# Sorting the edges of a four-layer graph network: column pieces of 96, 489, 489 and 489, each prepared right ahead of its ranks

## The reference, cut to what matters

```python
h = jnp.maximum(_layernorm(x, axis=-1), 0.0)
x = x + _L0_gnn_ref(h, src, dst, ...)                            # attention: softmax over the edges of a node
...
x = x + _L1_gnn_ref(h, ..., edge_index, edge_type_8)             # relations: means per type, in both directions
...
x = x + _L2_gnn_ref(h, edge_attr_16, ..., edge_index, 0, 4)      # sum over edges by src, then an MLP
...
x = x + _L3_gnn_ref(h, edge_index_t, edge_attr_6, ...)           # sum over edges by dst
```

## Time and profile before

| | us |
|---|---|
| time, median of 3 runs (15910.03 to 15919.94) | 15916.97 |
| time of the profiled execution | 15913.28 |
| its span | 15911.1 |
| busy: POOL / PE / DVE / PEld / ACT | 11144.0 / 10293.0 / 9384.4 / 8268.7 / 2592.3 |

### The profile page before, as it was taken

How to read it: one execution, slowest core, us unless ns; L and a number is a source line. 1 busy time by engine, 2 the same in 40 slices (tenths; PEclk the granted TensorE clock), 3 DMA queues, 4 the chain that set the end, 5 groups by cost and what they waited for, 6 DMA issues and landing times. The chain is left out here.

```text
span 15911.1 us, 207629 instructions
## 1 busy us (share of the span) xinstructions
PE 10293.0 (65%) x60197; PEld 8268.7 (52%) x60197; DVE 9384.4 (59%) x30337; ACT 2592.3 (16%) x6666; POOL 11144.0 (70%) x11474
## 2 busy tenths in 40 slices
PE   6766647777777775555554555553777768777777
PEld 2222226666666663344444444443666665666666
DVE  9977758888788777755555555554333332333331
ACT  0011114444444442211111111111000002000000
POOL 4777777777777776677777777774777760677773
PEclk9966669999999997755555555555555555555555
DMA  2011122222222224322223222223222232222223
GB/s 80 11 46 52 48 62 69 69 68 69 69 70 69 69 69 110 112 58 57 57 57 54 62 61 62 61 61 55 61 62 62 62 54 65 64 58 58 58 57 39
DMA packets 675304, 988.05 MB, mean 62 GB/s; under 512 B 232206, under 2 KB 473564, under 8 KB 674076
## 3 DMA queue, kind: packets, MB, share of 16 engines
q0 software_dynamic: 392896, 680.65, 18.5%
q1 hardware_dynamic: 281308, 294.11, 6.1%
HBM read 795.08 MB, written 178.86 MB: 61 GB/s over the span
## 5 line engine op out<-in xcount | busy, mean ns | idle before, releaser
L1528 DVE TENSOR_TENSOR acc<-banks,acc 128x145 f32 (+1 forms) x3328 | 1011.3, 304 | 2712.3 <-PE banks L1512 2345.9
L722 POOL DMA_INDIRECT far_sum_dst<-table_h,recs_sum_dst x1664 | 1578.1, 948 | 1026.0 <-DMA recs_sum_dst<-rec_dst 519.2
L621 POOL DMA_INDIRECT rec_dst<-stage_dst_sort,row_dst_sort x1563 | 1569.9, 1004 | 694.5 <-issue 475.6
L722 POOL DMA_INDIRECT far_sum_src<-table_h,recs_sum_src x1664 | 1576.5, 947 | 652.2 <-issue 426.3
L722 POOL DMA_INDIRECT far_att<-table_qv,recs_att x1664 | 1626.5, 977 | 532.5 <-issue 506.5
L722 POOL DMA_INDIRECT far_rel_dst<-table_xw,recs_rel_dst x1664 | 1590.0, 956 | 562.8 <-issue 506.9
L1404 DVE TENSOR_TENSOR acc<-banks,acc 128x128 f32 x3328 | 969.8, 291 | 1694.6 <-PE banks L1359 1331.7
L722 POOL DMA_INDIRECT far_rel_src<-table_xw,recs_rel_src x1664 | 1588.5, 955 | 537.4 <-issue 506.8
L1511 PE MATMUL banks<-far_sum_src,hot_sum_src 128*128 128x128 f32 x3328 | 1285.8, 490 | 745.7 <-issue 579.5
L1511 PE MATMUL banks<-far_sum_dst,hot_sum_dst 128*128 128x128 f32 x3328 | 1286.2, 490 | 640.4 <-issue 579.6
L1359 PE MATMUL banks<-far_rel_dst,hot_s_rel_dst 128*128 128x128 f32 x3328 | 851.4, 438 | 1045.1 <-DVE share_rel_dst L1394 708.2
(11 more groups left out here) (304 smaller groups left out, 23233.4 us busy)
## 6 DMA issues: line engine op xcount, KB each, us to landing
table_xw<-xw_rel_tables SPq DMA_DIRECT2D x98, 512.0 KB, 2.7
far_att<-table_qv,recs_att POOLq DMA_INDIRECT x1664
far_rel_dst<-table_xw,recs_rel_dst POOLq DMA_INDIRECT x1664
far_rel_src<-table_xw,recs_rel_src POOLq DMA_INDIRECT x1664
far_sum_src<-table_h,recs_sum_src POOLq DMA_INDIRECT x1664
far_sum_dst<-table_h,recs_sum_dst POOLq DMA_INDIRECT x1664
rec_dst<-stage_dst_sort,row_dst_sort POOLq DMA_INDIRECT x1563
rec_src<-moved_att,row_src POOLq DMA_INDIRECT x1248
```

The lines of the kernel that those rows point to most:

```text
L621: e.indirect_dma_start(out=flat_dst, out_offset=bass.IndirectOffsetOnAxis(ap=row["dst"][:, c + i:c + i + 1], axis=0), in_=stage["dst"][:, ...
L722: e.indirect_dma_start(out=self.far[:, g % RING, t, :], out_offset=None, in_=table, in_offset=bass.IndirectOffsetOnAxis(ap=index, axis=0)) ...
L1528: e.tensor_tensor(acc[:, bass.ds(at[t], 1), :], bank(g0, t).unsqueeze(1), acc[:, bass.ds(at[t], 1), :], ALU.add).then_inc(k.s_sum, 1)
```

## The change

The four quarters of 391, 391, 391 and 390 columns become four pieces of 96, 489, 489 and 489. The `begin`, parts and copies of a piece are no longer done for all columns at once ahead of all ranks, but for each piece right ahead of its 98 units. On TensorE the three rounds of a piece stand ahead of that piece's matmuls. GpSimd's chunk waits for the piece that holds its last column; 96 columns are three whole chunks.

```diff
-QUARTERS = 4
-QN = -(-ET // QUARTERS)
+PIECES = 4
+BEGINS = [0, *(96 + i * (ET - 96) // (PIECES - 1) for i in range(PIECES))]
+QN = max(b - a for a, b in zip(BEGINS, BEGINS[1:]))
...
-def quarter(q):
-
-    return q * QN, min(QN, ET - q * QN)
+def piece(q):
+
+    return BEGINS[q], BEGINS[q + 1] - BEGINS[q]
+
+
+def piece_of(c):
+    return sum(c >= b for b in BEGINS[1:])
...
+                def parted(q):
+
+                    c, m = piece(q)
+                    mine = begin[:, c:c + m]
+                    follow()
+                    then(e.scalar_tensor_tensor(out=mine, in0=mine, scalar=base[:, 0:1], in1=k.psum[q][0:W, 0:m], op0=ALU.add, op1=ALU.subtract))
+                    for j in range(3):
+                        follow()
+                        then(e.tensor_copy(part[:, j, c:c + m], mine))
+                        if j < 2:
+                            follow()
+                            then(e.tensor_tensor(mine, mine, part[:, j, c:c + m], ALU.subtract))
+                    at["parts", s, q] = n
+
+                    for g in range(GROUPS3):
+                        e.wait_ge(s_placed, (i * PIECES + q) * GROUPS3 + g + 1)
+                        e.tensor_copy(packed[:, g, c:c + m], k.psum[q][:, 0:m]).then_inc(s_packed, 1)
+
                 for u in range(AHEAD):
                     marked(u)
                 for u, (q, w) in enumerate(units):
-                    c, m = quarter(q)
+                    c, m = piece(q)
+                    if w == 0:
+                        parted(q)
...
                 for u, (q, w) in enumerate(units):
-                    c, m = quarter(q)
+                    c, m = piece(q)
+                    if w == 0:
+                        e.wait_ge(s_rank, at["parts", s, q])
+                        for g in range(GROUPS3):
+                            if g:
+                                e.wait_ge(s_packed, (i * PIECES + q) * GROUPS3 + g)
+                            for j in range(3):
+                                at0 = 3 * W3 * g - j + 2
+                                t = e.matmul(k.psum[q][:, 0:m], spread[:, at0:at0 + P], part[:, j, c:c + m], start=(j == 0), stop=(j == 2))
+                            t.then_inc(s_placed, 1)
+                        e.wait_ge(s_packed, (i * PIECES + q + 1) * GROUPS3)
...
-                e.wait_ge(s_row, (c + n - 1) // QN + 1)
+                e.wait_ge(s_row, piece_of(c + n - 1) + 1)
```

More of the change, by code:

```diff
@@ L245, in sort_edges @@
         spread, triple = sb("spread", [W, 3 * P], BF16), sb("triple", [P, W3 + 1], BF16)
-        over_part, over_packed = sb("over_part", [P, 3 * ET // 2 + 1]), sb("over_packed", [P, GROUPS3 * QUARTERS * QN // 2])
+        over_part, over_packed = sb("over_part", [P, 3 * ET // 2 + 1]), sb("over_packed", [P, -(-GROUPS3 * ET // 2)])
         begun = sb("begun", [P, ET])
@@ L250, in sort_edges @@
         part = over_part[0:W, :].bitcast(BF16)[:, 0:3 * ET].rearrange("w (j t) -> w j t", j=3)
-        packed = over_packed[:, :].bitcast(BF16).rearrange("p (g q n) -> p g q n", g=GROUPS3, q=QUARTERS)
+        packed = over_packed[:, :].bitcast(BF16)[:, 0:GROUPS3 * ET].rearrange("p (g n) -> p g n", g=GROUPS3)
         total = sb("total", [W, 1])
@@ L298, in sort_edges @@
         chunks = W // C7
-        units = [(q, w) for q in range(QUARTERS) for w in range(W)]
+        units = [(q, w) for q in range(PIECES) for w in range(W)]
         U = len(units)
@@ L347, in ranks @@
                 e.wait_ge(s_counted, (i + 1) * W)
-                for q in range(QUARTERS):
-                    c, m = quarter(q)
+                for q in range(PIECES):
+                    c, m = piece(q)
                     follow()
@@ L365, in ranks @@
                 then(e.tensor_scalar(base[:, :], k.psum[4][0:W, 0:1], float(P), None, ALU.mult))
-                follow()
-                for q in range(QUARTERS):
-                    c, m = quarter(q)
[L369 to L384, removed]
                 def marked(u):
                     q, w = units[u]
-                    c, m = quarter(q)
+                    c, m = piece(q)
                     if i * U + u >= 5:
@@ L414, in ranks @@
                                            op0=ALU.mult, op1=ALU.add).then_inc(s_row, 1)
-                e.wait_ge(s_row, QUARTERS * (i + 1))
+                e.wait_ge(s_row, PIECES * (i + 1))
                 if not i:
@@ L501, in tensor @@
                 e.matmul(k.psum[4][0:W, 0:1], k.before[0:W, 0:W], tiles[:, :], start=True, stop=True).then_inc(s_base, 1)
[L502 to L511, removed]
-                for u, (q, w) in enumerate(units):
-                    c, m = quarter(q)
+                for u, (q, w) in enumerate(units):
+                    c, m = piece(q)
+                    if w == 0:
[8 more added lines that the diff above has]
+                        e.wait_ge(s_packed, (i * PIECES + q + 1) * GROUPS3)
                     g, j = divmod(w, W3)
-                    if u == 0:
-                        e.wait_ge(s_packed, (i + 1) * GROUPS3 * QUARTERS)
                     e.wait_ge(s_begun, i * U + u + 1)
@@ L520, in tensor @@
                     bank = k.psum[4 + u % 4][:, 0:m]
-                    e.matmul(bank, triple[:, j:j + 1].to_broadcast([P, P]), packed[:, g, q, 0:m], start=True, stop=False)
+                    e.matmul(bank, triple[:, j:j + 1].to_broadcast([P, P]), packed[:, g, c:c + m], start=True, stop=False)
                     e.matmul(bank, before_b[:, :], mark[:, (i * U + u) % 5, 0:m], start=False, stop=True).then_inc(s_unit, 1)
```

## The result

The changed kernel takes 15951.27 us (median of 11 runs, 15937.88 to 15965.41), the kernel before in the same comparison 15916.5 us (11 runs, 15898.07 to 15943.88). The ratio is 1.0021, with a 95% interval of 1.0014 to 1.0029: slower by 35 us (22 to 46 by the interval), where 39 were forecast, 15956 from 15917. The profiled execution took 15953.65 us, with a span of 15951.9.

What follows compares the result with a forecast made beforehand. VectorE's `ranks`, then staging and 1083 writes, were taken to bound the sort. Terms of 3.3, 12.4, 2.8 and 1.5 made 20.0 us a side, +40 on 15917, less one: 15956, range 15938 to 15972.

Steps and rivals of the forecast that it cites:

- What bounds the sort: Sort's chain: VectorE's `ranks` until 826.83, 25.8 us of staging, then 1083 writes; first 480 writes beside it, 28 us slack.
- Parts, copies, refill: Preparing each piece on VectorE and TensorE: begins and parts +3.3, copies +12.4, refill +2.8 us a side.
- Units: VectorE's mark and copy pairs: wider and narrower units cancel, 38 against 38 us, leaving +1.5 us a side.
- floor: In 96-column units each copy waits for the copy before: 0.33 us where the line gives 0.31, +1.5 us a side.
- the line of 1.31 ns: Price per column of a VectorE unit: 489 columns take 0.13 us more than 391, 96 columns 0.39 less.
- The start: GpSimd's writes get their first rows at about 145, starting some 52 us earlier.
- The end: The early start all becomes waiting; the writes' end moves by +40 us, just as far as `normalize`.
- A: The forecast itself: `ranks` grows by 32 to 50 us and the end with it, 15949 to 15967; chance 0.61.
- B: Clock is up in TensorE's rounds and the floor is nothing: +22 us, 15939, up to 15949; chance 0.22.
- C: Small units on VectorE don't overlap: 0.46 us instead of 0.33, adding 25 us, 15981; chance 0.09.
- D: GpSimd's earlier start carries through to the end: 52 us less, 15865; chance 0.05.
- E: Nothing moves: more than half of the added waits in `ranks` are hidden, 15917 to 15939; chance 0.03.

Runs made afterwards that it cites:

- e1: Changed kernel with GpSimd's writes held back until the second piece has its rows; 15956.75 us, ratio 1.0023 to the kernel before.
- e12: Changed kernel with all pieces' begins up front and a piece's three spread rounds in three banks without waits between; 15946.06 us, ratio 1.0013 to the kernel before.
- e7: As e12, plus unused matmuls on TensorE ahead of the later pieces' rounds, on the chip running 28% longer; ratio 0.9988 to the kernel before.
- e10: Kernel before with pieces of 96, 489, 489, 489, all prepared up front, and 17 chunks staged ahead instead of 14; 15863.29 us, ratio 0.9969.
- e11: Kernel before with only 17 chunks staged ahead of the first window instead of 14; 15904.58 us, ratio 0.9985.
- e3: Changed kernel with four equal pieces, each still prepared right ahead of its ranks; 15945.61 us, ratio 1.0017 to the kernel before.

## Why the prediction was right

**What bounds the sort.** Right: VectorE's `ranks`, then staging, then the writes. 826.83 to 864.98 is +38.15, and the writes resume +37.98. e1 confirms the slack on the other side: 92 us of later start moved the resumption by 1.2. The stop was forecast at some 120 us and took 116.65.

**Parts, copies, refill: +18.5 a side forecast.** The preparation from the first begin to the first copied unit took 106.94 to 126.24 before, 19.3 us. After, it is 4.4 at the small piece and 11.07, 11.00 and 11.07 at the wide ones, 37.5 together: +18.2. On side `src` it is 18.7 before and 37.7 after: +19.0. The single terms hold too. Parts of a wide piece: 148.73 to 152.28, 3.55 (3.5). Copies 2.17 and 0.78 apart (2.18 and 0.78), at the clock of 0.50 that was assumed. Refill 158.12 + 0.67 to 159.88, 1.09 (1.10). The handoff of 0.28 that the earlier trace rows gave and the copy are what three banks take away from between the rounds (e12); the higher clock takes the rest (e7). Two slips change nothing in the sum: a side has 15 more instructions for begins and parts (24 in place of 9), not 18, and 96 writes take 125 us at the pace of the earlier trace rows, not 121.

**Units: +3.0 forecast for both sides; +1.1 measured, as a sum of misses.** The other rows of the two sides of `ranks` (units and row numbers) grew by 3.0 on side `dst` and shrank by 1.9 on `src`. With 18.2 and 19.0 of preparation, and 0.2 less between the sides, that makes the 38.15. The small unit takes 0.367 (143.48 to 143.85), not 0.33: a mark starts 0.17 behind a copy, and a copy 0.20 behind a mark. This 0.20 is the same at 96, 391 and 489 columns, and the three units, 0.367, 0.70 and 0.813, lie on one line of 1.13 to 1.15 ns a column. So no floor shows at 96 columns. What was off is the line of 1.31 ns: it charged the mark's 0.26 ns a column, which cost nothing. By the measured line the small units save 98 x 0.333 and the wide ones cost 294 x 0.113, again nothing, 0.6 us.

Writes beside them do matter. Wide units without writes took 0.813, in the last piece of `src`, where GpSimd stands still from 774 on; beside writes, in the second piece of `dst`, they took 0.845. e1 shows that the writes are the cause: its writes begin behind that second piece, whose units take 0.812 there, and they run beside its last piece of `src`, whose units take 0.844. So the new stop gives about 3 us back. The prediction had called this nothing, within 2.

**The start.** Forecast 145, measured 149.72. 98 units x (0.367 - 0.33) are 3.6 of the 4.7 us.

**The end.** It was to move as far as `normalize`. It moved by 32.1, not by 38: from the resumption to the memset 1420.3 us pass, before 1426.2. Further waits for staging are 2.9 of these 5.9 us: 31.7 less 28.03 before, 117.4 less 116.65 after. The other 3.0 are in the writes themselves: these 1083 are busy for 1086.0 us, before for 1089.0, and in other runs for 1084 to 1091; why was not looked into. The prediction's sign that the writes' end moves just as far as `normalize` was thus off by 5.9. The span grew by 40.8, of which 8.7 lie behind the sort; runs of one kernel differ by more than that.

**The rivals.** The time alone does not part A from B, whose upper end, 32 us above the kernel before, lies within the interval of 22 to 46; the trace does. B needed the higher clock in the rounds; the window 154 to 156 shows 0.50, and the copies are 2.17 apart. C needed 0.46 for a small unit, and it took 0.367: the mark starts at 143.65 while the copy before it is busy until 143.75. The Trainium skill's drain rule (VectorE: DVE Perf Modes, "The DRAIN you can't avoid"), taken alone, would have had the mark wait; the same section says that a next instruction that is not held starts earlier, and the trace agrees with that at 96 columns too. D, the early start that reaches the end, was wrong here and right in e10 against e11, by the end of the sort: it needed another condition than the one that I named. I had put it at `ranks` ending 81 us sooner; three more staged chunks do the same. E fell with `normalize`, which is 38.15 us later, and with e3.

## What to carry to other kernels

Ahead of starting a stream of work sooner, ask what it meets: here it met a staging stop, and an earlier start turned into a longer wait until three more chunks were staged in front. The largest wait in an engine's list may be worth nothing while one a sixth of its size decides, and once that is gone a cut of the large one counts: 33.3 us less of it ended e10's sort 34.2 us sooner than e11's. Work that is cut in pieces pays its pipeline's filling for each piece: here each round behind the first cost 0.95 us more in a shared bank than in one of its own, and the matmuls behind TensorE's idle time ran at half its clock, unless it was given work to do until then (e7).

## What the runs showed of the hardware

- A mark and a copy in turn on VectorE: 0.367 us for 96 columns, 0.70 for 391, 0.813 for 489. That is a slope of 1.13 to 1.15 ns a column; the 0.20 from mark to copy is the same at all three widths, so the mark's width costs nothing where it overlaps the copy.
- TensorE's granted clock stayed at 0.50 through the 36 us of small units; in the window from 120 to 130 the profile shows it busy for 9.27 of 10 us (the ends of its matmuls are modelled). In the wide units from 170 to 240 it was 1.00, with 48.75 of 70 us busy. The half clock cost next to nothing in the small units: behind the first one a single copy of side `dst` waited for TensorE, 0.37 us. What keeps the clock down there was not tested.
- Wide units on VectorE were 4% longer beside GpSimd's indirect writes, one of 128 rows each 1.3 us: 0.845 against 0.812 in the same piece of after and e1.
- One chip ran the same programs 28% longer, with waits of 4.7 to 4.9 us put down to "remote" between TensorE's matmuls and VectorE's copies.
